# An attention loop's PSUM banks in two rings, its value rounds in two places, and the maxima's split on GpSimd

## The reference

```python
xn = _layernorm(x)
# attention: 16 heads of 8, lifted to a latent of 32 per head
q_lat = rope(q @ q2l_w.T + q2l_b);  k_lat = rope(k @ kv2l_w.T + kv2l_b);  v_lat = v @ kv2l_w.T + kv2l_b
q_for_k = q_lat @ wqk_w.T + wqk_b
att = softmax(where(causal, einsum('bhql,bhkl->bhqk', q_for_k, k_lat) * L ** -0.5, -inf))
y = (einsum('bhqk,bhkl->bhql', att, v_lat) @ l2o_w.T + l2o_b) -> [8, 512, 128]
attn = y @ cproj_w.T + cproj_b
# experts: sigmoid router, the best of 7 per token, and a shared one
ffn = 0.5 / total_weight * shared_out + switched / total_weight
return x + attn + ffn
```

## Time and profile before

| what | value |
|---|---|
| time, median of 3 runs (lowest, highest) | 630.9 us (629.06, 633.19) |
| span of the profiled execution | 623.4 us; the runs' median is 7.5 us above it, for what lies around the span |
| busy: TensorE, VectorE, GpSimd, ScalarE | 575.2, 484.2, 365.7, 358.8 us |
| first and last 512-wide value round of the steady loop in the chain of waits | 158.17 and 508.34 us |
| transfers | 98.01 MB, 157 GB/s on average |

### The profile page before, as it was taken

How to read it: one execution, slowest core, us unless ns; L and a number is a source line. 1 busy time by engine, 2 the same in 40 slices (tenths; PEclk the granted TensorE clock), 3 DMA queues, 4 the chain that set the end, 5 groups by cost and what they waited for, 6 DMA issues and landing times.

```text
span 623.4 us, 13018 instructions
## 1 busy us (share of the span) xinstructions
PE 575.2 (92%) x3642; PEld 399.2 (64%) x3642; DVE 484.2 (78%) x1708; ACT 358.8 (58%) x888; POOL 365.7 (59%) x477
## 2 busy tenths in 40 slices
PE   4998789689999999999999999999999998999993
PEld 4766576456566566666655666656565554899992
DVE  6498556578899998988898988988986777677772
ACT  4863243126777777767676777676776665332320
POOL 3303767456676676666675756766764323377775
PEclk9999899768999999999999999999999999999997
DMA  9535556677877777877777767777787863133332
GB/s 288 215 135 177 173 166 206 156 170 172 191 181 178 171 181 191 189 175 171 189 171 171 178 148 174 185 167 183 150 194 167 224 193 107 44 34 31 35 32 25
DMA packets 51370, 98.01 MB, mean 157 GB/s; under 512 B 7154, under 2 KB 26482, under 8 KB 51174
## 3 DMA queue, kind: packets, MB, share of 16 engines
q1 hardware_dynamic: 33344, 71.92, 48.9%
q10 hardware_dynamic: 11462, 20.64, 10.1%
q0 software_dynamic: 6496, 4.62, 5.7%
HBM read 26.40 MB, written 19.87 MB: 74 GB/s over the span
## 4 chain that ended last, share of the span: by engine, by line
PE 51%; DMA 9%; POOL 9%; issue 5%; ACT 2%; DVE 2%; SPq 2%; ACTq 0%; POOLq 0%; DVEq 0%
PE bank L1437 14%; PE bank L1422 13%; PE bank L1329 12%; POOL out L1145 7%; DMA KQ<-dkq 6%; PE bank L1347 4%; PE bank L1445 3%; PE bank L1486 2%; DMA out<-ye,token 1%; DMA KQ<-mxT 1%; PE bank L1493 1%; SPq L1055 1%; PE bank L1465 1%; ACT prob L1289 1%; ACT dkq L1159 1%
## 5 line engine op out<-in xcount | busy, mean ns | idle before, releaser
L1622 DVE CUSTOM_DVE_ANT_0 scratch<-bank,late 128x512 bf16<-128x512 f32 (+3 forms) x512 | 234.1, 486 | 32.6 <-PE bank L1422 25.7
L1289 ACT ACTIVATE prob<-bank 128x512 f32<-128x512 f32 (+3 forms) x512 | 205.0, 438 | 75.1 <-PE bank L1437 73.8
L1437 PE MATMUL bank<-KQ 98*128 98x256 f32 (+2 forms) x512 | 183.0, 375 | 5.9 <-ACT prob L1289 4.1
L1134 POOL TENSOR_SCALAR_AFFINE_SELECT prob<-prob 128x256 f32<-128x256 f32 x256 | 106.3, 418 | 116.0 <-ACT prob L1289 115.6
L1422 PE MATMUL bank<-KQ 96*128 96x256 f32 (+2 forms) x512 | 165.4, 373 | 2.3 <-DVE mx L1622 1.5
L1437 PEld LDWEIGHTS bank<-KQ 98*128 98x128 f32 x512 | 96.4, 190 | 71.4 <-ACT prob L1289 54.5
L1422 PEld LDWEIGHTS bank<-KQ 96*128 96x128 f32 x512 | 97.8, 194 | 55.7 <-issue 28.0
L1329 PE MATMUL bank<-prob,v_all 128*9 128x256 f32 (+3 forms) x1024 | 92.4, 435 | 0.9 <-POOL prob L1134 0.9
L1145 POOL DMA_INDIRECT out<-ye,token x38 | 59.3, 1561 | 33.1 <-issue 17.4
L1347 PE MATMUL bank<-stk,wl 96*128 96x512 f32 x120 | 52.2, 443 | 3.5 <-PEq L286 2.3
L359 POOL DMA_INDIRECT sorted_x<-xn,pos x32 | 32.0, 1001 | 39.1 <-DVEq L824 30.2
(11 more groups left out here) (171 smaller groups left out, 929.8 us busy)
## 6 DMA issues: line engine op xcount, KB each, us to landing
KQ<-dkq SPq DMA_DIRECT2D x192, 256.0 KB, 3.9
stk<-latent ACTq DMA_DIRECT2D x39, 256.0 KB, 4.7
latent<-qkH SPq DMA_DIRECT2D x8, 512.0 KB
latent<-qkL SPq DMA_DIRECT2D x8, 512.0 KB
sorted_x<-pad_sb SPq DMA_DIRECT2D x10, 260.0 KB, 3.7
stk<-latent SPq DMA_DIRECT2D x9, 256.0 KB, 4.5
x<-in_x SPq DMA_DIRECT2D x8, 256.0 KB, 5.8
out<-x SPq DMA_DIRECT2D x8, 256.0 KB, 2.3
```

What stands on the lines that cost most here:

```text
L1134: nc.gpsimd.affine_select(out=diag, in_=diag, compare_op=ALU.is_ge, fill=0.0, base=0, pattern=[[0, 2], [1, P]], channel_multiplier=-1).the ...
L1289: nc.scalar.activation(prob[:, n % 4, cell, at:at + PW[j]], ST[i % 2][:, lo - q0:T - q0], ACT.Exp, scale=SCALE).then_inc(exp_done, 1)
L1437: nc.tensor.matmul(ST[b][:, 0:T - q0], KQ[0:SROWS, 0, n % SLOTS, T * b + P * j:T * b + P * (j + 1)], KQ[0:SROWS, 1, n % SLOTS, T * b + q0: ...
L1622: nc.vector.tensor_tensor_reduce(scratch[:, i % 2, 0:w], S[k % SBANKS][:, 0:w], mask[:, T - w:T], 1.0, MASKED, ALU.add, ALU.max, mx[:, m % ...
```

## The change

The banks are handed out by two rings. `BankRing.take` gives the next bank in turn and what must have been read before it is written again. Scores and projections go round banks 0, 1, 2 and 6; T tiles, maxima, row sums, latent products and the products of a turn round banks 3, 4 and 7. The readers look up the bank under the tile's name in `home`. TensorE's function now stands first in the block, because it fills `home`; its text is otherwise moved unchanged but for the lines below. The value rounds of a pair are issued as three in a row (512, 128 and 256 columns, before index 11 of the even step) and one (384, before index 4 of the odd step), where they had four places. ScalarE only copies the transposed maxima out of PSUM, into the new `mxR`, and GpSimd makes the high and the low part. All order tables have new values. `high_q` has the wait for the fills that `high_k` has. `xsH` and `xsL` of the experts lie in the memory of `KQ`.

```diff
-SBANKS = 3
+SCORE_BANKS = (0, 1, 2, 6)
+KEY_BANKS = (3, 4, 7)
-TENSOR_ORDER = ('SSTSTTTSSTSTSTST', 'SSSTTTSTSTTSSSTT')
-MAX_T_AT, PROJECT_AT, YT_AT, LATENT_AT, SUMS_AT, OUT_AT = ((4, 3), ((6, 16), (4, 16)), (8, 14), (12, 13),
-                                                           (1, 9), (6, 5))
-VALUES_AT = {(0, 5): ((2, True, False),),
-             (0, 8): ((3, False, False),),
-             (1, 2): ((0, False, False),),
-             (1, 5): ((1, False, True),)}
-MAX_LOW_AT, OUT_ADD_AT, ROPE_AT, SUMS_USED_AT = (2, 2), (3, 3), ((5, 8), (2, 8)), 5
-MAX_HIGH_AT, Y_COPY_AT, YT_COPY_AT, HIGH_K_AT, HIGH_Q_AT = (1, 0), (1, 6), 4, ((4, 6), (3, 3)), (6, 6)
+TENSOR_ORDER = ('SSTTSSTSSTTSTSTT', 'SSTSTTTSSTSSTSTT')
+MAX_T_AT = (2, 2)
+PROJECT_AT = ((7, 16), (1, 16))
+YT_AT = (15, 0)
+LATENT_AT = (8, 12)
+SUMS_AT = (1, 2)
+OUT_AT = (16, 14)
+VALUES_AT = {(0, 11): ((0, True, False), (3, False, False), (2, False, False)), (1, 4): ((1, False, True),)}
+OUT_ADD_AT = (5, 8)
+ROPE_AT = ((4, 8), (0, 8))
+SUMS_USED_AT = 0
+MAX_COPY_AT = (0, 0)
+SPLIT_AT = (-1, -1)
+Y_COPY_AT = (1, 5)
+YT_COPY_AT = 7
+HIGH_K_AT = ((5, 8), (3, 4))
+HIGH_Q_AT = (4, 4)
+POOL_WORK = {(0, -1): ('low_k', 1, 1),
+             (0, 1): ('add_q', 1, 1),
+             (0, 2): ('low_q', 1, 0),
+             (1, 1): ('add_k', 0, 0),
+             (2, -1): ('add_k', 0, 1),
+             (2, 1): ('low_q', 1, 1),
+             (2, 3): ('add_q', 0, 0),
+             (3, 1): ('low_k', 0, 0)}
...
+            def free_bank(ring, key, reader):
+
+                home[key], before = ring.take(reader)
+                if before is not None:
+                    pe.wait_ge(*before)
+                return bank[home[key]]
...
+                into = free_bank(score_ring, ("P", G, part, ab), (pa_used, use + 1))
...
+                into = free_bank(score_ring, ("S", m, i), (s_max, k + 1))
...
+                into = free_bank(key_ring, ("T", n, i), (exp_done, k + 1))
...
+                into = free_bank(key_ring, ("wq", G, f), (qf_ready, 2 * (G - 1) + f + 1))
...
+                        into = free_bank(key_ring, ("mx", m), (mxT_copied, m + 1))
...
+                        into = free_bank(key_ring, ("z", pair), (z_used, pair + 1))
...
+            def split_maxima(m):
+
+                pool.wait_ge(mxT_copied, m + 1)
+                if m >= 2:
+                    pool.wait_ge(mx_in[m % 2], 32 * (m // 2))
+                nc.gpsimd.tensor_copy(mxT[:, m % 2, 0, :], mxR[:, m % 2, :]).then_inc(mxT_high, 1)
+                pool.wait_ge(mxT_high, m + 1)
+                nc.gpsimd.tensor_tensor(mxT[:, m % 2, 1, :], mxR[:, m % 2, :], mxT[:, m % 2, 0, :].bitcast(F32),
+                                        ALU.subtract).then_inc(mxT_low, 1)
+
             def turn(n, slot):
 
                 G, part = chunk(n)
-                if (part, slot) in WORK:
-                    op, back, f = WORK[part, slot]
+                if slot == SPLIT_AT[n % 2] and 0 <= n + 1 < STEPS:
+                    split_maxima(n + 1)
+                if (part, slot) in POOL_WORK:
+                    op, back, f = POOL_WORK[part, slot]
...
             def high_q(G, f):
 
                 half = slice(T * f, T * (f + 1))
+                if G >= 2 and f == 0:
+                    for m in range(HG * (G - 2), HG * (G - 1)):
+                        act.wait_ge(filled[m % SLOTS], 48 * (m // SLOTS + 1))
                 act.wait_ge(wq_ready, 2 * (G - 1) + f + 1)
...
-                    if i == MAX_HIGH_AT[n % 2] and 0 <= m < STEPS:
+                    if i == MAX_COPY_AT[n % 2] and 0 <= m < STEPS:
                         act.wait_ge(mxT_ready, m + 1)
                         if m >= 2:
-                            act.wait_ge(mx_in[m % 2], 32 * (m // 2))
-                        nc.scalar.copy(mxT[:, m % 2, 0, :], MXT).then_inc(mxT_high, 1)
+                            act.wait_ge(mxT_low, m - 1)
+                        nc.scalar.copy(mxR[:, m % 2, :], bank[home["mx", m]][0:2 * QT, 0:P]).then_inc(mxT_copied, 1)
...
-                    if i == MAX_LOW_AT[n % 2] and 0 <= m < STEPS:
-                        dve.wait_ge(mxT_high, m + 1)
-                        nc.vector.tensor_tensor(mxT[:, m % 2, 1, :], MXT, mxT[:, m % 2, 0, :].bitcast(F32),
-                                                ALU.subtract).then_inc(mxT_copied, 1)
...
+class BankRing:
+
+    def __init__(self, banks):
+        self.banks, self.readers, self.turn = banks, {}, 0
+
+    def take(self, reader):
+
+        at = self.banks[self.turn % len(self.banks)]
+        self.turn += 1
+        before = self.readers.get(at)
+        self.readers[at] = reader
+        return at, before
```

More of the change, by code:

```diff
@@ L936, in attention @@
               const_row, sorted_x, out, under, base_out):
+    _, xsH, xsL = under(("before_xs", [P, (SLOTS - 2) * PT], F32), ("xsH", [C, 2, P], F32R), ("xsL", [C, 2, P], F32R))
     _, g1 = under(("before_g1", [P, (SLOTS - 1) * PT], F32), ("g1", [P, 2, I], F32))
@@ L968, in attention @@
     wqk, wqk_b, lat_b = late[:, LATE["wqk"]], late[:, LATE["wqk_b"]], late[:, LATE["lat_b"]]
[L970 to L977, removed]
+    Y, M = bank[5], bank[7]
+    score_ring, key_ring = BankRing(SCORE_BANKS), BankRing(KEY_BANKS)
+    home = {}
     y_clear, minus_set, ones_set = sem("y_clear"), sem("minus_set"), sem("ones_set")
@@ L1104, in low_q @@
                                         ALU.subtract).then_inc(ql_ready, 1)
[L1106 to L1113 removed]
+            OPS = {"add_k": add_k, "add_q": add_q, "low_k": low_k, "low_q": low_q}
+            def split_maxima(m):
[6 more added lines that the diff above has]
+                                        ALU.subtract).then_inc(mxT_low, 1)
             def turn(n, slot):
                 G, part = chunk(n)
[L1118 to L1119 removed]
+                if slot == SPLIT_AT[n % 2] and 0 <= n + 1 < STEPS:
+                    split_maxima(n + 1)
+                if (part, slot) in POOL_WORK:
+                    op, back, f = POOL_WORK[part, slot]
                     if live(G - back):
[L1121 to L1126 removed]
+                        OPS[op](G - back, f)
+            for step, slot, op, f in sorted((HG * back + part, slot, op, f)
+                                            for (part, slot), (op, back, f) in POOL_WORK.items()):
+                if step < HG:
+                    OPS[op](1, f)
             for n in range(FIRST, LAST):
@@ L1271, in _ @@
                             act.wait_ge(out_ready, 2 * pair + f)
-                        nc.scalar.copy(yT[:].rearrange("c (t p) -> c t p", t=QT), M[:].rearrange("c (p t) -> c t p", t=QT)
+                        nc.scalar.copy(yT[:].rearrange("c (t p) -> c t p", t=QT),
+                                       bank[home["yt", pair, f]][:].rearrange("c (p t) -> c t p", t=QT)
                                        ).then_inc(ynT_copied, 1)
@@ L1550, in rope @@
                 dve.wait_ge(pa_ready, 8 * (G - 1) + 2 * part + ab + 1)
-                nc.vector.scalar_tensor_tensor((t1, t2)[ab][:, half], projected(G, part, ab)[:], lat_b[:, kd:kd + 1], (cosr, sinr)[ab],
-                                               ALU.add, ALU.mult).then_inc(pa_used, 1)
+                nc.vector.scalar_tensor_tensor((t1, t2)[ab][:, half], bank[home["P", G, part, ab]][:], lat_b[:, kd:kd + 1],
+                                               (cosr, sinr)[ab], ALU.add, ALU.mult).then_inc(pa_used, 1)
             def low_xT(t):
@@ L1594, in _ @@
                         rows = xres[:, QT * f:QT * (f + 1), :].rearrange("p t c -> p (t c)")
-                        nc.vector.tensor_tensor(rows, rows, M[:], ALU.add).then_inc(o_added, 1)
+                        nc.vector.tensor_tensor(rows, rows, bank[home["o", pair, f]][:], ALU.add).then_inc(o_added, 1)
                     for ab in range(2):
@@ L1600, in _ @@
                     if i == SUMS_USED_AT and pair is not None:
-                        Z = M[:].rearrange("p (t h c) -> p t h c", t=2 * QT, h=2)
+                        Z = bank[home["z", pair]][:].rearrange("p (t h c) -> p t h c", t=2 * QT, h=2)
                         dve.wait_ge(z_ready, pair + 1)
```

417 lines of the change are left out of this document (193 added, 224 removed).

## The result

The changed kernel takes 641.28 us (median of four runs, 639.53 to 642.29), the kernel before 630.33 (four runs, 629.06 to 633.19): a ratio of 1.0182, 95% interval 1.0136 to 1.0228. It is slower by 1.8%. The prediction said 628.0, with a range of 603 to 645.

What follows compares the result with a forecast made beforehand. The attention loop was taken as bound by TensorE's queue, next by a VectorE–TensorE loop: 23.39 against 23.55 per four steps, 2.5 us less; span about 620.5 plus 7.5 gives 628, range 603 to 645.

Steps and rivals of the forecast that it cites:

- The step that failed: GpSimd's split of the maxima: they leave some 0.4 later but are made at place 2, so no net cost.
- with 0.3 of room behind it: `high_q` at place 4, n % 4 = 0: last fill lands 5.9 after issue begins, when ScalarE arrives, 0.3 to spare.
- six turns between batch pairs (about 13.3): In the old kernel's chain, pairs alternate 11.98 and 11.57 us, apart from six turns of about 13.3.
- Rival 2: GpSimd's split is dear, 1.7 instead of 0.7, delaying maxima and fills: 31 us more, 659; chance 0.15.
- The walk of 1 us later maxima: In rival 2: maxima and fills 1 us later make `high_q`, T0 and adds late, 2 us in four steps.
- the merged block: TensorE's three value rounds in a row, even step: 1.65 with one switch, against 2.47 apart, saving 0.62 per pair.
- the split's price: GpSimd's copy and subtraction of 8x128 per step: 0.7 together, between a cheap end of 0.4 and a dear 1.7.
- the loop by VectorE and TensorE: Attention loop: VectorE's maxima and ropes and TensorE's order limit pairs to 11.50 short, 11.89 long; 23.39 per four steps.
- the waits before projection 7 and the latent product: TensorE would stand before projection 7 for VectorE, and before every fourth step's latent for GpSimd, 0.39 more.
- nearly all eaten: Merged rounds' 0.62 per pair hardly shortens the loop: the short pair goes only from 11.57 to 11.50.
- rival 3: Loop closes as forecast, but small waits (maxima at T0, `low_k`) add 0.6 in four steps: 637; chance 0.15.
- The sum: Four steps 23.39 against 23.55, 15.5 times: 2.5 us less; span 623.4 to about 620.5, plus 7.5: 628.

Runs made afterwards that it cites:

- y1: Changed kernel with each fill transfer from the sixth step on cut to its first quarter, same instructions otherwise: 616.46 us, ratio 0.9819.
- y3: Changed kernel without GpSimd's copy and subtraction of the maxima; SP sends ScalarE's copy for both rows: 620.73 us, ratio 0.9889.
- z2: Changed kernel with one row of maxima, rounded by ScalarE's copy, no low part and no GpSimd split: 618.34 us, ratio 0.9833.
- y2: Kernel before the change with fill transfers from the sixth step on cut to their first quarter: 619.68 us, ratio 0.9854.
- z1: Changed kernel with SP issuing the fill of step n + 4 ahead of the maxima of step n + 1: 719.22 us, ratio 1.1491.
- x2: Changed kernel with GpSimd's `low_q` of the first half moved one step later, away from in front of the split: 649.35 us, ratio 1.0358.
- y4: x2 with the odd step's first rope at VectorE's place 2 instead of place 0: 650.62 us, ratio 1.0355.

## Why the prediction was wrong

| kernel | transposition to SP's maxima, median us | four steps | time | ratio to before |
|---|---|---|---|---|
| before | 1.01 | 23.50 | 630.3 | 1 |
| changed | 1.94 | 24.08 | 641.3 | 1.0182 |
| changed, quarter fills (y1) | 1.91 | 23.29 | 616.5 | 0.9819 |
| changed, no split (y3) | 0.59 | 23.29 | 620.7 | 0.9889 |
| changed, one row (z2) | 0.59 | 23.28 | 618.3 | 0.9833 |

The forecast was a kernel some 0.4% faster; it became 1.8% slower.

- **The step that failed** is in the part on GpSimd: "so the maxima leave some 0.4 later, but they are made at place 2 instead of 4 and 3: together zero". It counted the split's own 0.7 and not what stands ahead of it in GpSimd's queue. Behind the transposition the maxima leave 0.93 later in the median and 1.5 later in the step behind `low_q` (2.81 against 1.33), and each fill goes out behind them: there it leaves 6.4 us ahead of its reader, where it left 7.9 and needs 6.9. Taking the split away gives 20.5 us back (y3), taking the fills' landing away 24.8 (y1).
- **With it fell "with 0.3 of room behind it".** `high_q` stood for a fill in 8 places, 9.9 us, and T5 behind it. The prediction walked this fill from the odd step's maxima, without GpSimd's queue. That S itself would stand for a fill (15.0 us on the weight loads, 7.2 on the matmuls) is in no part of it. A sign of it was in the trace of the kernel before: the chain has two plain pairs of 13.25 and 13.13, which the prediction's "six turns between batch pairs (about 13.3)" pass over, and in them `high_k` waits 2.21 and 2.09 us for a fill, not 0.94.
- **Rival 2 had the place and the chain right, but the wrong condition**: "It decides from about 1.1 us per split". The split cost 0.78 and the chain closed all the same, for it is delay that counts, and 1.4 us of it (305.0 to 306.42 in the step shown) came from `low_q` and a cut. The walk of 1 us later maxima there (2 us in four steps) was two and a half times the 0.79 between 24.08 and 23.29, and twice the 1.00 that the seven plain groups differ by in the mean. The Trainium skill's advice that the prediction put beside it ("Perfetto Trace Analysis", Optimizing GPSIMD Operations) doesn't decide this case: with VectorE in place of GpSimd the time was 662.87.
- **Right**: the merged block (1.65, measured 1.63), the split's price (0.7, 0.78), the loop by VectorE and TensorE (11.50 and 11.89, measured 11.43 and 11.86 once no fill is late), the waits before projection 7 and the latent product, and that the 0.62 per pair would be "nearly all eaten". Four steps without late fills are 23.29 against 23.15 for the kernel before without them (y1, y2): in the plain steps rings and merged rounds won nothing. `low_k`, in rival 3, is part of the chain above, but as the end of a late fill.
- **The sum.** (2.5 off the span of 623.4 is 620.9, not 620.5; nothing hangs on it.) From first to last transposition the changed kernel needs 24.9 more than y1 (392.95 and 368.06). Of these, three long steps give 8.0 (9.72, 10.50 and 9.45 against 7.03, 7.40 and 7.19), the last six steps 8.7 (38.55 against 29.87), the seven plain groups 7.0 and all other steps 1.2. So late transfers cost most where other loads run beside them, at places for which the prediction has no term, and some of it is the lower clock. With fills on time the kernel takes 618 to 621, not 628: from first to last transposition z2 needs 371.2 where the kernel before needs 379.1. Of these 7.9 the seven plain groups give 3.7 (163.2 and 167.0), and most of the rest lies at the turns and in the last six steps, which the prediction left at nothing.

## What to carry to other kernels

When work moves to another engine, price its place in that engine's queue, not only its length: add up what can stand ahead of it, and follow what is queued behind its result on the next engine, here transfers of 768 KB behind 8 KB. A transfer that the profile of before shows as waited for now and then (0.94 in one step of four, at times 2.2) has little room left, so look up how far ahead of its reader it leaves and how long it takes. And ask first whether the small product is needed at all: here the low part of a maximum that softmax cancels cost more than the new order won.

## What the runs showed that was not expected

- For 8 KB asked for behind 768 KB on SP's queue T0 stood until 3.5 us after the end of their issue, 64.8 us in all (z1). In the changed kernel, with the maxima in front, T0's weight loads stood for them 3.4 us.
- An engine at 64% (GpSimd) and one at 73% (VectorE) had no place to give for these moves: moving one instruction of 1.28 by one step cost some 8 us (x2), and moving a rope by two places beside it replaced one wait of VectorE (8.4 us) by another (10.7 to 19.6 us) and won nothing (y4).
- Behind four stands of TensorE of some 1 to 2 us in the changed kernel the granted clock fell to 0.5 for 3 to 7 us, behind two of 1.1 and 2.4 it didn't; in the kernel before it was 1.00 from 160 to 530 us.
